# First experts: the short chunk of the second product on two row tiles of 64, and five banks in rotation for the first

## What is computed

```python
hg = jnp.einsum('th,ehi->eti', xf, wg)                 # 128 -> 176
hu = jnp.einsum('th,ehi->eti', xf, wu)                 # 128 -> 176
eo = jnp.einsum('eti,eih->eth', jax.nn.silu(hg) * hu, wd)   # 176 -> 128
y = jnp.einsum('te,eth->th', wdense, eo)
shared = jax.nn.silu(xf @ swg) * (xf @ swu) @ swd
x = x + attention0(xn) + (y + shared)
```

## Time and profile before

| | us |
|---|---|
| median of 3 runs | 919.67 (919.15 to 921.34) |
| the profiled execution, its own time | 917.82 |
| its span, first to last instruction | 916.3 |
| TensorE busy | 838.1 (91%) |
| VectorE busy | 701.6 (77%) |
| GpSimd busy | 625.9 (68%) |
| ScalarE busy | 572.2 (62%) |

### The profile page before, as it was taken

The page is one execution under the profiler, slowest core; times in us unless marked ns, Lnnn a source line. Parts: engine busy times, 40 slices in busy tenths (PEclk is TensorE's granted clock), DMA queues, the critical chain, the costliest instruction groups (busy, mean ns, idle before and its releaser), DMA issues.

```text
span 916.3 us, 22375 instructions
## 1 busy us (share of the span) xinstructions
PE 838.1 (91%) x7975; PEld 746.4 (81%) x7975; DVE 701.6 (77%) x1809; ACT 572.2 (62%) x1183; POOL 625.9 (68%) x607
## 2 busy tenths in 40 slices
PE   3789999999899999997998889888998899999997
PEld 3678878989799999985665566566898899999997
DVE  7687787886577998887898997897653556567786
ACT  5766465444466667769887776663664567566652
POOL 4157676777305888777888887886777777767663
PEclk9999999999999999999999999998999999999999
DMA  9799992115658998962111111116586778799996
GB/s 263 228 407 404 396 397 95 50 53 170 239 152 274 309 323 259 288 193 66 40 40 40 38 38 43 40 41 226 182 266 202 242 257 261 266 306 334 365 359 190
DMA packets 130990, 191.06 MB, mean 209 GB/s; under 512 B 15808, under 2 KB 85952, under 8 KB 130752
## 3 DMA queue, kind: packets, MB, share of 16 engines
q1 hardware_dynamic: 96720, 141.21, 46.1%
q0 software_dynamic: 16640, 34.37, 11.2%
q10 hardware_dynamic: 17520, 14.06, 4.8%
HBM read 110.74 MB, written 80.97 MB: 209 GB/s over the span
## 4 chain that ended last, share of the span: by engine, by line
PE 47%; DVE 23%; POOL 9%; issue 7%; DMA 6%; ACT 4%; SPq 4%; DVEq 0%; POOLq 0%; ACTq 0%
PE pair L888 11%; PE pair L835 4%; PE pair L834 4%; PE pair L836 4%; POOL sent L2014 3%; PE pair L755 3%; PE pair L865 3%; POOL ex_joined L2025 3%; DVE a_en L1578 2%; PE pair L668 2%; DVE X L1511 2%; PE pair L675 2%; DMA ex_stage<-in_experts 2%; DVE stats_t L1146 2%; PE pair L677 2%
## 5 line engine op out<-in xcount | busy, mean ns | idle before, releaser
L2014 POOL DMA_INDIRECT sent<-a_rows,slot x224 | 220.8, 986 | 81.1 <-issue 56.6
L2116 POOL DMA_INDIRECT back<-ex_tile_out,address x136 | 151.8, 1117 | 59.5 <-issue 32.6
L2025 POOL DMA_INDIRECT ex_joined<-outs,slot x128 | 132.7, 1036 | 81.7 <-DMA outs<-ex_tile_out 45.9
L834 PE MATMUL pair<-ex_x_hi,ex_w_hi 128*128 128x256 f32 x497 | 147.7, 297 | 0.0
L835 PE MATMUL pair<-ex_x_lo,ex_w_hi 128*128 128x256 f32 x497 | 141.7, 285 | 0.0
L836 PE MATMUL pair<-ex_x_hi,ex_w_lo 128*128 128x256 f32 x497 | 141.4, 285 | 0.0
L888 PE MATMUL pair<-ex_stage,ex_hid 128*128 128x128 f32 x1136 | 132.5, 275 | 0.0
L888 PEld LDWEIGHTS pair<-ex_stage,ex_hid 128*128 128x128 f32 x1136 | 129.9, 192 | 0.0
L1714 ACT ACTIVATE ex_w_hi<-ex_stage 128x768 fp32r<-128x768 f32 (+1 forms) x72 | 67.5, 937 | 91.0 <-DMA ex_stage<-in_experts 91.0
L1840 ACT ACTIVATE ex_hid<-pair,ex_stage 128x256 f32<-128x256 f32 x284 | 107.1, 498 | 0.1
L1349 DVE TENSOR_TENSOR ex_w_lo<-ex_stage,ex_w_hi 128x768 fp32r<-128x768 f32 (+1 forms) x72 | 77.4, 1075 | 36.2 <-ACT ex_w_hi L1714 35.6
(11 more groups left out here) (246 smaller groups left out, 1986.0 us busy)
## 6 DMA issues: line engine op xcount, KB each, us to landing
ex_stage<-in_experts SPq DMA_DIRECT2D x72, 578.0 KB, 5.6
outs<-v_heads SPq DMA_DIRECT2D x8, 4352.0 KB, 33.2
ex_stage<-in_experts SPq DMA_DIRECT2D x72, 320.0 KB, 4.9
ex_tile_in<-sent SPq DMA_DIRECT2D x72, 128.0 KB
outs<-ex_tile_out SPq DMA_DIRECT2D x71, 128.0 KB
ex_joined<-back ACTq DMA_DIRECT2D x15, 512.0 KB, 8.0
ex_tile_in<-sent SPq DMA_DIRECT2D x54, 132.0 KB
X<-in_x SPq DMA_DIRECT2D x16, 256.0 KB, 5.3
```

The lines of the kernel that those rows point to most:

```text
L834: pe.matmul(o[:, of_half], wh, x_hi[i % 2][:, of_half], start=True, stop=False)
L2014: pool.indirect_dma_start(out=sent[layer], out_offset=bass.IndirectOffsetOnAxis(ap=slot_i[layer][k][:, s, j:j + 1], axis=0), in_=rows[laye ...
L2025: pool.indirect_dma_start(out=joined[g % NJOIN][:, j, k, :], out_offset=None, in_=outs, in_offset=bass.IndirectOffsetOnAxis(ap=slot_i[0][k ...
L2116: pool.indirect_dma_start(out=back, out_offset=bass.IndirectOffsetOnAxis(ap=address[i % NSIDE][:, s // HALF, s % HALF:s % HALF + 1], axis= ...
```

## The change

1. The second product. The weights' last 48 rows are padded to 64 and stand twice in the 128 partitions, in rows 0 to 63 and 64 to 127. `down0` multiplies, for each half, the two blocks' chunk 0 on all 128 rows, one into bank 6 and one into bank 7, and then both blocks' chunk 1 on 64 rows each: block 0 on rows 0 to 63 into bank 6, block 1 on rows 64 to 127 into bank 7. The number of matmuls stays at 8 for a tile of two halves.
2. `hidden0` writes chunk 1 of `hid` in two instructions of 48 partitions and 256 columns, block 0's part to partitions 0 to 47 and block 1's to 64 to 111.
3. `results0` copies from the two banks 6 and 7 in one instruction, with the same 128x512 elements.
4. The first product rotates over banks 0 to 4 (`up_bank`), the transposes and the next layer's early work move from bank 6 to bank 5. The waits for banks stand ahead of each of the three products instead of ahead of all, and `q_of(0)` and `k_of(0)` wait for the last tile's first `silu` and first `hid`.

The diff, without the places where only a 6 becomes a 5 in a call (`rows_to_columns`, `split_rows`, `transposes`, `columns`):

```diff
 def logits_bank(layer, step):
-    return 6 if layer == 0 or step == 1 else 2
+    return 6 if layer == 0 else 5 if step == 1 else 2
 
...
 def ranks_bank(layer, step):
-    return 0 if layer == 0 else 6 if step == 1 else 3
+    return 0 if layer == 0 else 5 if step == 1 else 3
 
...
 
+        def up_bank(n, j):
+
+            return bank[(3 * n + j) % 5]
+
         def returns(i):
...
 
-            def banks_of_up0(n):
+            def up0(n):
+                pe.wait_ge(w_lo_here, n + 1)
+                pe.wait_ge(x_lo_here, n + 1)
                 if n == 0:
                     pe.wait_ge(q0_ready, NG)
                     pe.wait_ge(k0_ready, 2 * NG)
-                elif n == 1:
-                    pe.wait_ge(sh_ready, 3 * NG)
-                else:
+                if n >= 2:
+                    pe.wait_ge(hid_ready, 2 * (n - 2) + 1)
+                product(up_bank(n, 0), n, 0).then_inc(up_done, 1)
+                if n >= 2:
                     pe.wait_ge(hid_ready, 2 * (n - 2) + 2)
-
-            def up0(n):
-                b = 3 * (n % 2)
-                pe.wait_ge(w_lo_here, n + 1)
-                pe.wait_ge(x_lo_here, n + 1)
-                banks_of_up0(n)
-                product(bank[b], n, 0).then_inc(up_done, 1)
-                product(bank[b + 1], n, F0P + 64).then_inc(up_done, 1)
-                product(bank[b + 2], n, P).then_inc(up_done, 1)
+                product(up_bank(n, 1), n, F0P + 64).then_inc(up_done, 1)
+                if n >= 1:
+                    pe.wait_ge(act_done, 2 * (n - 1) + 1)
+                product(up_bank(n, 2), n, P).then_inc(up_done, 1)
 
...
                 pe.wait_ge(hid_ready, 2 * n + 2)
-                for i in range(HALF * halves(n)):
-                    for c in range(2):
-                        m = pe.matmul(bank[7][:, i * C:(i + 1) * C], hid[n % 2][c][:, i * P:(i + 1) * P],
-                                      stage[0][n % NSTAGE[0]][:, i // HALF, 2 * F0P + c * C:2 * F0P + (c + 1) * C], start=(c == 0), stop=(c == 1))
+                for h in range(halves(n)):
+                    w = stage[0][n % NSTAGE[0]][:, h, 2 * F0P:2 * F0P + 2 * C]
+                    for i in range(HALF):
+                        pe.matmul(bank[6 + i][:, h * C:(h + 1) * C], hid[n % 2][0][:, (HALF * h + i) * P:(HALF * h + i + 1) * P], w[:, 0:C],
+                                  start=True, stop=False)
+                    for i in range(HALF):
+                        part = slice(64 * i, 64 * i + 64)
+                        m = pe.matmul(bank[6 + i][:, h * C:(h + 1) * C], hid[n % 2][1][part, h * P:(h + 1) * P], w[part, C:2 * C],
+                                      start=False, stop=True)
                 m.then_inc(down_done, 1)
...
                 if n in EX_COLUMNS:
-                    transposes(1, EX_COLUMNS[n], 6)
+                    transposes(1, EX_COLUMNS[n], 5)
                 if n == EX_SUMS:
                     logits_by_columns(1, 1, 0).then_inc(sums_done, 1)
                 if n == EX_LOGITS:
-                    sums_to_rows(6, 0, GPS, sums_ex).then_inc(logits_done, GPS)
+                    sums_to_rows(5, 0, GPS, sums_ex).then_inc(logits_done, GPS)
                 if n == EX_RANKS:
...
                 else:
-                    pe.wait_ge(hid_ready, 2 * (NTILES - 1))
+                    pe.wait_ge(act_done, 2 * (NTILES - 1) + 1)
                 twice = len(COLUMNS[1].get(g + LEAD - 1, ())) > 1
...
                     pe.wait_ge(u1_ready, g)
+                else:
+                    pe.wait_ge(hid_ready, 2 * (NTILES - 1) + 1)
                 pe.matmul(bank[1], w_attn1[:, C:2 * C], flat(xTg(g)), start=True, stop=True).then_inc(k1_done, 1)
...
             def hidden0(n, c):
-                b = 3 * (n % 2)
-                k = (P, F0T)[c]
-                a = slice(0, SLOTS * halves(n))
-                up = bank[b + 1][0:P, a] if c == 0 else bank[b + 2][64:64 + F0T, a]
+                k = halves(n)
+                a = slice(0, SLOTS * k)
                 dve.wait_ge(act_done, 2 * n + c + 1)
                 dve.wait_ge(up_done, 3 * n + 2 + c)
                 if n >= 2:
                     dve.wait_ge(down_done, n - 1)
-                dve.tensor_tensor(hid[n % 2][c][0:k, a], gate_s[c][0:k, a], up, ALU.mult).then_inc(hid_ready, 1)
+                if c == 0:
+                    m = dve.tensor_tensor(hid[n % 2][0][:, a], gate_s[0][:, a], up_bank(n, 1)[:, a], ALU.mult)
+                else:
+                    gate, up = (t.rearrange("p (h i t) -> p h i t", i=HALF, t=P) for t in (gate_s[1][0:F0T, a], up_bank(n, 2)[64:64 + F0T, a]))
+                    for i in range(HALF):
+                        m = dve.tensor_tensor(blocks(hid[n % 2][1][64 * i:64 * i + F0T, 0:k * P]), gate[:, :, i, :], up[:, :, i, :], ALU.mult)
+                m.then_inc(hid_ready, 1)
 
...
             def silu(n, c):
-                b = 3 * (n % 2)
                 k = (P, F0T)[c]
                 act.wait_ge(up_done, 3 * n + 1 + 2 * c)
                 if n >= 1:
                     act.wait_ge(hid_ready, 2 * (n - 1) + c + 1)
                 a = slice(0, SLOTS * halves(n))
-                act.activation(gate_s[c][0:k, a], bank[b + 2 * c][0:k, a], ACT.Silu).then_inc(act_done, 1)
+                act.activation(gate_s[c][0:k, a], up_bank(n, 2 * c)[0:k, a], ACT.Silu).then_inc(act_done, 1)
 
...
                 act.wait_ge(down_done, i + 1)
-                a = slice(0, SLOTS * halves(i))
-                act.activation(flat(tile_out[i % NOUT][:])[:, a], bank[7][:, a], ACT.Copy).then_inc(out_ready, 1)
+                k = halves(i)
+                by_bank = tile_out[i % NOUT][:, 0:HALF * k, :].rearrange("p (h i) c -> p i h c", i=HALF)
+                act.activation(by_bank, blocks(pair[3][:], 512)[:, :, 0:k * C].rearrange("p i (h c) -> p i h c", c=C), ACT.Copy).then_inc(out_ready, 1)
 
...
                     if step == LEAD:
-                        columns(1, EX_LATER[0], 6)
+                        columns(1, EX_LATER[0], 5)
                     keys_by_token(g)
...
 
-    wd = padded_rows(i["L0_ffn_wd"], 2 * P)
+    wd = i["L0_ffn_wd"]
+    tail = padded_rows(wd[:, P:], P // 2)
     wu = i["L0_ffn_wu"]
-    experts0 = np.concatenate([padded(i["L0_ffn_wg"], F0P), padded(wu[:, :, P:], 64), wu[:, :, 0:P], wd[:, 0:P], wd[:, P:2 * P]], axis=2)
+    experts0 = np.concatenate([padded(i["L0_ffn_wg"], F0P), padded(wu[:, :, P:], 64), wu[:, :, 0:P], wd[:, 0:P], np.concatenate([tail, tail], axis=1)], axis=2)
     w2 = i["L1_ffn_w2"].reshape(E, NC1, P, C).transpose(0, 2, 1, 3).reshape(E, P, NC1 * C)
```

More of the change, by code:

```diff
@@ L956, in tensor_program @@
                 if n + 1 < NTILES:
-                    rows_to_columns(0, n + 1, 6)
+                    rows_to_columns(0, n + 1, 5)
                 if n < NTILES:
@@ L966, in tensor_program @@
                     down0(n - 1)
-            transposes(1, EX_LATER[0], 6)
+            transposes(1, EX_LATER[0], 5)
             def v_of(g):
@@ L1530, in vector_program @@
                     split_weights(0, n + 1)
-                    split_rows(0, n + 1, 6)
+                    split_rows(0, n + 1, 5)
                 if n < NTILES:
@@ L1876, in scalar_program @@
                 if n in EX_COLUMNS:
-                    columns(1, EX_COLUMNS[n], 6)
+                    columns(1, EX_COLUMNS[n], 5)
                 if n in EX_ROWS:
```

## The result

| | before | after |
|---|---|---|
| median, us (10 runs each) | 919.66 (917.50 to 924.47) | 927.29 (925.82 to 929.34) |
| profiled execution, its own time | 917.82 | 926.16 |
| its span | 916.3 | 924.7 |

The ratio is 1.0065 (95% interval 1.0044 to 1.0086): slower by 4.0 to 7.9 us. The two medians lie 7.6 us apart; the ratio is an estimate from all executions and not their quotient (1.0083), and in the table of the experiments too the two differ by up to 0.2%. The forecast was 927.6.

A forecast was written before the change was run, and what follows sets the result against it. TensorE was taken to bound the first experts' stage: 10.3 us more work less 2.4 absorbed gives 7.9, so 925.7 for the profiled execution, 927.6 on the median's scale. Own range 923.9 to 930.0; wider range 920 to 934.

The forecast's parts named there:

- The slots: Second product: 8 instructions on 64 rows run two abreast in 4 slots, saving 0.45 us per tile.
- The two rivals in which the pair does not run abreast: Second product: pair takes 3 slots of 4, 933.6 us, or nothing overlaps, 939.9 us; chance 0.07.
- The changes of tiling: Second product and following transposes: four changes between 128 and 64 rows cost 0.74 us per tile.
- The rivals of free changes: Second product: changes between 128 and 64 rows cost nothing, so the kernel gains 7.3 us, 912.4; chance 0.10.
- a price near 0.11: Second product: at this price per change TensorE's gain and loss cancel, VectorE adds 2 us, 921; chance 0.07.
- The period: TensorE's time per tile in the first experts' stage: 4.66 us in place of 4.37 up to tile 17.
- What gives: First experts' stage: 2.4 us of TensorE's 10.3 more is absorbed, of at most 6.1 us of waits for VectorE.
- The shift of the first gather: GpSimd's first gather, 7 tiles into the stage, comes 2 us later.
- The wait for gathered rows: VectorE's waits for gathered rows in the stage, 2.5 us in three times, shrink by 1.7 us.
- VectorE's split: 48-row multiplication in two: 0.15 us more a tile, counting instead of 0.29 in five heavy tiles with next-layer jobs.
- The banks and waits at nothing: Bank rotation and later waits cost nothing; without the cover, up to one silu a tile, 0.60 us.
- Behind the stage: Everything after the first experts' stage hangs on one chain of waits and so moves as a whole.

The follow-up runs named there:

- e12: Kernel after with both blocks' chunk 1 on rows 0 to 63, one behind the other, hid in one instruction; 935.60 us against 922.29 before, ratio 1.0135.
- e10: Kernel after with all chunk 0 products first, then all pairs: two changes of tiling a tile, not four; 919.59 us against 921.36 before, ratio 0.9985.
- e9: The kernel after, unchanged, timed again on another chip; 927.92 us against 921.36 before, ratio 1.0076.
- e11: Kernel after with chunk 1 on 128 zero-padded rows, hid in one instruction, plus one unread product a tile; 925.42 us against 922.29 before, ratio 1.0016.
- e1: Kernel after with chunk 1 on 128 zero-padded rows again and hid in one instruction; 1019.70 us against 1018.79 before, ratio 1.0022.
- e5: Same kernel as e1, run again; 1019.06 us against 1019.17 before, ratio 1.0003.
- e2: Same kernel as e12, on a slow chip; 1024.8 us against 1018.79 before, ratio 1.0043.
- e7: Same kernel as e2, run again on a slow chip; 1024.56 us against 1019.17 before, ratio 1.0065.
- e8: Same kernel as e11, on a slow chip; 1022.12 us against 1019.17 before, ratio 1.0035.

## Why the prediction was right

**The slots.** Forecast: two abreast, 0.45 us saved a tile. Shown by e12: without the pair the period is 0.43 us longer (5.10 and 4.67). The two rivals in which the pair does not run abreast fall.

**The changes of tiling.** Forecast 0.74 us for four, taken over from tiles of 32 rows and 32 columns. Measured 0.75 after, 0.74 in e12, 0.36 for two in e10. The rivals of free changes and of a price near 0.11 fall: 0.18 to 0.19 each. Only its place was off: I had all 0.74 ahead of the next transposes' start (2.08 us), while it is 2.02 us there and the last 0.07 falls behind it. The Trainium skill, page "TensorEngine Tiling (Array Packing)", section Tiling Modes, has a change of mode drain the engine. These rows agree with it for 128 and 64 rows in that each change costs time, 0.18 to 0.19 us; that it is a drain they do not show.

**The period.** Forecast 4.66, measured 4.67, and 35 x 0.30 = 10.5 us for 10.3.

**What gives.** Forecast 2.4 us, measured 2.7, and the stage +7.9 forecast, +7.6 (after, without its half-clock stretch) and +8.0 (e9). That the sum came out is in part luck, for its two parts were off in opposite directions. The shift of the first gather was forecast as 2 us; the timeline of GpSimd after has it here, 2.7 us later than in the earlier trace rows, of which 1.1 us is the stage's later start and 1.6 the tiles:

```profile
285.55 0.99 POOL L2038 DMA_INDIRECT ex_joined<-outs,slot  x1 [47.34 <-PE pair L672]
```

The wait for gathered rows went altogether (2.5 us, I took 1.7). The other way, VectorE's split was mis-sized: I let its 0.15 us count in five heavy tiles, 0.75 us. e9 and e11 differ by 2.6 us of stage (8.0 and 5.4), 1.0 of it by the period (35 x 0.03) and 1.6 by TensorE's waits for VectorE (3.4 and 1.8). So the split costs about 1.6 us, twice my term, and this excess of 0.85 us nearly cancels the 0.8 us that I had too little for the gathered rows. The 1.6 rests on two profiled executions; no run that can show it timed the split alone.

**The banks and waits at nothing.** Agrees: no wait of TensorE for `silu` or a bank appears in its waits after, e1 and e5 took the time of before, and e11 is at most 1.0038.

**Behind the stage.** Forecast: it moves as a whole. The profiles do not bear that out to the microsecond. Here is each span in three, by the first and the last start of the second product:

| profile | ahead, us | stage, us | behind, us | span, us |
|---|---|---|---|---|
| before | 253.2 | 161.9 | 501.2 | 916.3 |
| after | 254.3 | 171.3 | 499.1 | 924.7 |
| e9 | 256.8 | 169.9 | 497.4 | 924.1 |
| e10 | 256.6 | 163.8 | 502.0 | 922.4 |
| e11 | 253.6 | 167.3 | 498.1 | 919.0 |
| e12 | 257.0 | 180.8 | 499.2 | 937.0 |

Ahead of the stage these executions differ by up to 3.8 us (the last section has what goes with it) and behind it by up to 4.6, without an order that follows the edits. After, the span grew by 1.1 + 9.4 - 2.1 = 8.4 us. So the mechanism and the stage's size are shown, but that the forecast of 927.6 met the median of 927.29 within 0.3 us is luck: the interval of the ratio alone is 4 us wide. The clock is a likely part of the difference behind the stage: here is 620 to 720 us before, and then after, the figure ahead of the DMA share being the clock:

```profile
620.00:720.00 100.00, 87.73 (x863) 81.86 (x862) 56.95 (x138) 50.66 (x111) 75.03 (x73) 0.92 0.66 222
```

```profile
620.00:720.00 100.00, 89.52 (x961) 81.71 (x953) 62.61 (x155) 55.25 (x118) 78.06 (x74) 0.97 0.61 204
```

Before had 8 points of its 100 us, 16 us, at 1.2 GHz there, and after 6 us. Such stretches fall elsewhere in each execution; a difference of one or two microseconds between two profiles says nothing.

## What to carry to other kernels

Count changes of tiling before slots: on these fp32 products a change cost 0.18 to 0.19 us and a slot is 0.11, so a change must save about 1.7 slots to pay, and the same products ordered with two changes a tile instead of four gave back 8 us of 928. Work put on the engine that bounds a stage is paid only as far as that engine did not wait already (here its waits took up 2.7 to 6.1 us of the added 10 to 26), and an edit on the second engine can eat that slack, by two profiles about 1.6 us of it here. When an ordering is the loss, the first variant to try is the one with all parts of a kind together.

## What was not expected of the hardware

- On two of the chips the same kernel takes 1019 us and not 920. The second product's 16 instructions there took 3.37 instead of 1.95 us in e5's row, and 5% of the chain is put down to another core or an unknown queue. Edits that add 10 to 26 us on TensorE (e2, e7, e8) moved the time by 3 to 7 us.
- The stage opened at 1.2 GHz for part of the time in all four profiles with the 64-row form on the chips of 920 us, and in neither without it, although no 64-row product had run yet. From 246 to 256 us the granted clock was 0.83 after and 0.66 in e9, e10 and e12, with 1.00 before and in e11, and the first second product started at 254.3, 256.8, 256.6 and 257.0 against 253.2 and 253.6 us. Here is that stretch in e9 and in e11.

```profile
246.00:256.00 10.00, 7.59 (x41) 7.41 (x42) 5.82 (x10) 5.80 (x9) 0.00 (x0) 0.66 0.50 137
```

```profile
246.00:256.00 10.00, 8.09 (x69) 7.68 (x68) 8.63 (x13) 7.45 (x12) 0.00 (x0) 1.00 0.44 121
```

The 64-row form is not what it takes: in e1, which has none, the clock was 0.83 in the ten microseconds ahead of the stage, whose first second product starts at 279.5 us:

```profile
266.00:276.00 10.00, 8.15 (x56) 7.89 (x56) 3.96 (x6) 3.81 (x6) 0.00 (x0) 0.83 0.46 132
```

What does go with it in the six profiles is how long TensorE stood idle just ahead, until the rows of a tile had landed: 2.06, 2.20, 2.11 and 2.01 us where the clock fell behind it (after, e9, e10, e12), 1.63 and 1.79 us where it did not (before, e11). Here are the transposes behind that wait in e9 and in e11:

```profile
246.79 0.63 PE L672 MATMUL pair<-consts,ex_tile_in 128*128 128x128 f32 x4 [2.20 <-DMA ex_tile_in<-sent]
```

```profile
245.65 0.62 PE L672 MATMUL pair<-consts,ex_tile_in 128*128 128x128 f32 x4 [1.79 <-DMA ex_tile_in<-sent]
```

In all six a second wait of 1.6 us follows. No run changed the first wait alone, so that it sets the clock is not shown.
